# Held-out products in the middle of the value parts, three sign tiles moved to ScalarE, and the sum of a head's parts behind a later tile

## The reference

```python
q_proj, k_proj = one scalar per token and head (two linear layers with a gelu, then centred and scaled)
Z = concatenate(k_proj, q_proj); sort; cumsum; unsort
context = 2 * sum_k relu(Zq - Zk) * (v_k - mean v)        # what the sorted sums come to
norm    = sum_k |Zq - Zk|, at least 1e-4
out     = context / norm
```

## Time and profile before

| what | us |
|---|---|
| median of three runs | 1379.29 (1377.48 to 1381.62) |
| the profiled execution | 1386.35 |
| its span | 1385.0 |
| PE busy in it | 1080.4 (78%) |
| DVE busy in it | 960.1 (69%) |
| ACT busy in it | 818.6 (59%) |
| POOL busy in it | 354.9 (26%) |
| ACT sign tiles, 224 | 429.9 |
| DVE sign tiles, 288 | 352.7 |
| PE matmuls on the signs, 8192 | 398.3 |

### The profile page before, as it was taken

One profiled execution on the slowest core, in us unless ns is written; L12 is line 12 of the kernel. 1 busy time (PEld: TensorE's weight loads), 2 busy tenths in 40 slices (PEclk: granted clock), 3 DMA queues, 4 the chain that ended last, 5 costly groups with the idle time before them and its releaser, 6 DMA issues. The chain is left out here.

```text
span 1385.0 us, 30980 instructions
## 1 busy us (share of the span) xinstructions
PE 1080.4 (78%) x12566; PEld 932.0 (67%) x12566; DVE 960.1 (69%) x1709; ACT 818.6 (59%) x957; POOL 354.9 (26%) x381
## 2 busy tenths in 40 slices
PE   5365689798898899979998897665548948983797
PEld 3254686598888887658888886554348845652797
DVE  5111686889999995889999996255626647843465
ACT  7111454699999954489999996143413326660332
POOL 3745001100000000200004401571644421345344
PEclk9689699899999999979999999795669979966799
DMA  8953400311212100012123213554243450013343
GB/s 252 340 149 122 157 1 0 74 63 63 93 63 94 63 2 0 4 62 94 63 74 113 90 67 101 199 199 145 89 135 104 120 179 1 1 47 108 112 119 100
DMA packets 83824, 133.72 MB, mean 97 GB/s; under 512 B 14083, under 2 KB 70403, under 8 KB 79043
## 3 DMA queue, kind: packets, MB, share of 16 engines
q1 hardware_dynamic: 65440, 91.27, 20.9%
q0 software_dynamic: 12960, 35.60, 7.1%
q10 hardware_dynamic: 5286, 4.88, 1.1%
HBM read 84.18 MB, written 47.54 MB: 95 GB/s over the span
## 5 line engine op out<-in xcount | busy, mean ns | idle before, releaser
L1655 ACT ACTIVATE b_signs<-b_q_everywhere,normed 128x2048 bf16<-128x2048 f32 x224 | 429.9, 1993 | 13.4 <-PE banks L1537 13.0
L1537 PE MATMUL banks<-b_value_parts,b_signs 128*128 128x102 bf16 x8192 | 398.3, 209 | 46.1 <-DVE b_signs L1872 39.6
L1537 PEld LDWEIGHTS banks<-b_value_parts,b_signs 128*128 128x128 bf16 x8192 | 377.9, 98 | 64.4 <-DVE b_signs L1872 49.1
L1872 DVE TENSOR_SCALAR b_signs<-b_q_everywhere,normed 128x2048 bf16<-128x2048 f32 x288 | 352.7, 1279 | 4.7 <-PE banks L1537 4.6
L850 POOL DMA_INDIRECT moe_slots<-normed,slot_of_token x128 | 135.7, 1060 | 39.1 <-issue 35.2
L1924 POOL MEMSET b_value_parts<- 128x256 bf16 x2 | 2.6, 1310 | 404.6 <-PE banks L1385 404.6
L415 PE MATMUL banks<-identity 128*128 128x128 f32 x264 | 45.7, 351 | 53.7 <-issue 24.3
L379 DVE BATCH_NORM_STATS2 ln_stats<-residual 128x6 f32<-128x256 f32 x192 | 71.4, 417 | 17.1 <-SPq L2147 9.7
L415 PEld LDWEIGHTS banks<-identity 128*128 128x128 f32 x264 | 44.2, 264 | 54.5 <-issue 33.5
L406 ACT ACTIVATE normed<-residual,ln_shift,ln_rstd 128x256 f32<-128x256 f32 x128 | 67.9, 592 | 11.9 <-DVE ln_shift L401 11.8
L487 PE MATMUL banks<-identity,normed 128*128 128x128 f32 x256 | 51.8, 338 | 25.5 <-ACT normed L406 21.1
(11 more groups left out here) (292 smaller groups left out, 2299.3 us busy)
## 6 DMA issues: line engine op xcount, KB each, us to landing
b_q_everywhere<-q_rows SPq DMA_DIRECT2D x32, 1024.0 KB
normed<-expert_rows SPq DMA_DIRECT2D x6, 1024.0 KB, 10.0
d_rows<-moe_slots SPq DMA_DIRECT2D x39, 129.5 KB
f_rows<-moe_slots SPq DMA_DIRECT2D x39, 129.5 KB
moe_slots<-a_empty SPq DMA_DIRECT2D x8, 518.0 KB, 10.3
a_rows<-moe_slots SPq DMA_DIRECT2D x16, 259.0 KB
c_rows<-moe_slots SPq DMA_DIRECT2D x16, 259.0 KB
expert_rows<-a_empty SPq DMA_DIRECT2D x1, 4096.0 KB
```

Of the source, the lines that this page charges most:

```text
L1537: ins = nc.tensor.matmul(banks[qt // QPB][:, qt % QPB * VP:(qt % QPB + 1) * VP], t.SG[:, (hh * TB + kt) % RING, qt * P:(qt + 1) * P], t.VO ...
L1655: nc.scalar.activation(t.SG[:, g % RING, :], t.QB[:, hh % 2, :], ACT.Sigmoid, bias=t.NKT[:, kt, hh % H:hh % H + 1], scale=STEEP).then_inc( ...
L1872: nc.vector.tensor_scalar(t.SG[:, g % RING, :], t.QB[:, hh % 2, :], t.KTM[:, kt, hh % H:hh % H + 1], 1.0, ALU.is_gt, ALU.mult).then_inc(s. ...
```

## The change

`WARM_SENT` goes from 16 to 28 and `WARM_ROWS` from 12 to 16. In heads 6, 12 and 15 tile 15 is made by ACT and not by DVE. The sum of a head stands behind tile 4 and not tile 2 of the next head. The fifth context step of head 15 stands behind the loop, ahead of the last sum. The held-out matmuls stand in `pe_parts` at n = 2, with DVE's five operations at n = 4 of its loop over the pairs, and three new blocks of 8 idle matmuls stand in `pe_parts` at n = 4, 6 and 8, in bank 4. ACT gets one small sigmoid behind its first six copies of the parts.

```diff
-WARM_SENT, WARM_ROWS, WARM_HEADS, WARM_PAIR = 16, 12, 28, 4
+WARM_SENT, WARM_ROWS, WARM_HEADS, WARM_PAIR, WARM_PARTS = 28, 16, 28, 4, 8
-DVE_KT = tuple(t for t in range(TB) if t not in ACT_KT)
+EVEN_HEADS = (6, 12, H - 1)
+def act_tiles(h):
+    return ACT_KT + (TB - 1,) if h in EVEN_HEADS else ACT_KT
+def dve_tiles(h):
+    return tuple(t for t in range(TB) if t not in act_tiles(h))
+def act_made(hh):
+    return sum(len(act_tiles(i % H)) for i in range(hh))
+def dve_made(hh):
+    return TB * hh - act_made(hh)
@@ sp_attention
-                nc.sync.wait_ge(s.sign_d, len(DVE_KT) * (hh - 1))
-                nc.sync.wait_ge(s.sign_a, len(ACT_KT) * (hh - 1))
+                nc.sync.wait_ge(s.sign_d, dve_made(hh - 1))
+                nc.sync.wait_ge(s.sign_a, act_made(hh - 1))
@@ pe_parts, the end of the loop over n
+        if n == 2:
+            pe_held(k, batch)
+        if n in (4, 6, 8):
+            if n == 4:
+                nc.tensor.wait_ge(s.held, batch + 1)
+            pe_warm(k, k.bank[4], WARM_PARTS)
@@ pe_held
-    nc.tensor.wait_ge(s.nkt, batch + 1)
     nc.tensor.wait_ge(s.qtm, batch + 1)
+    nc.tensor.wait_ge(s.ones_set, batch + 1)
+    nc.tensor.wait_ge(s.kz_third, batch + 1)
@@ pe_head
-        nc.tensor.wait_ge(s.ones_set, batch + 1)
-        nc.tensor.wait_ge(s.kz_third, batch + 1)
-        pe_held(k, batch)
     if hh >= 2:
         nc.tensor.wait_ge(s.sum, hh - 1)
-    if h == 1:
-        nc.tensor.wait_ge(s.held, batch + 1)
@@ act_prepare, ahead of the loop over the pairs
+    nc.scalar.activation(t.ZS[:, 1:2], k.EPS[0:H, 0:1], ACT.Sigmoid)
     for n in range(PAIRS + 1):
@@ dve_attention
-            for kt in DVE_KT:
+            for kt in dve_tiles(h):
                 dve_sign(k, hh, kt)
-                if h == 0 and kt == 6:
-                    dve_held(k, batch)
-                if h and kt == 2:
+                if h and kt == 4:
                     dve_sum(k, hh - 1)
                 for group in made:
-                    if kt in CONTEXT_KT:
+                    if kt in CONTEXT_KT and (h, kt) != (H - 1, CONTEXT_KT[-1]):
                         dve_context(k, batch, group, CONTEXT_KT.index(kt))
...
+        dve_context(k, batch, len(TOGETHER) - 2, len(CONTEXT_KT) - 1)
         dve_sum(k, batch * H + H - 1)
@@ dve_prepare, in the loop over the pairs
+        if n == 4:
+            dve_held(k, batch)
         if n == 2:
```

More of the change, by code:

```diff
@@ L1531, in pe_head @@
                                  t.HELD3[:, h, :].unsqueeze(1).broadcast_to([P, QPB, 6]), start=False, stop=False)
-        if kt in ACT_KT:
-            nc.tensor.wait_ge(s.sign_a, len(ACT_KT) * hh + ACT_KT.index(kt) + 1)
+        if kt in act_tiles(h):
+            nc.tensor.wait_ge(s.sign_a, act_made(hh) + act_tiles(h).index(kt) + 1)
         else:
-            nc.tensor.wait_ge(s.sign_d, len(DVE_KT) * hh + DVE_KT.index(kt) + 1)
+            nc.tensor.wait_ge(s.sign_d, dve_made(hh) + dve_tiles(h).index(kt) + 1)
         for qt in range(TB):
@@ L1576, in act_attention @@
         for h in range(H):
-            for kt in ACT_KT:
+            for kt in act_tiles(h):
                 act_sign(k, batch * H + h, kt)
@@ L1729, in dve_prepare @@
             if i == 0 and batch:
-                nc.vector.wait_ge(s.sign_a, len(ACT_KT) * H * batch)
+                nc.vector.wait_ge(s.sign_a, act_made(H * batch))
             z = t.Z[:, q, ch * BANK:(ch + 1) * BANK]
@@ L1865, in dve_sign @@
     g = hh * TB + kt
-    if kt == DVE_KT[0]:
+    if kt == 0:
         nc.vector.wait_ge((s.qb_in0, s.qb_in1)[hh % 2], 16 * (hh // 2 + 1))
```

## The result

The kernel after took 1370.39 us (median of 5 runs, 1366.56 to 1371.59), the one before 1380.7 in the same comparison (5 runs). The ratio is 0.9937, 95% interval 0.9921 to 0.9952, so 8.7 us faster, 6.6 to 10.9. Against 1379.3 that is 1370.6: faster, as forecast, and 3.6 us short of the forecast, inside the range. The profiled execution took 1370.63, its span 1369.4.

The account below looks back on a forecast made before the run. DVE was taken to bound the heads, ACT those at a batch's start. Savings of 5.6 and 7.4 us made 13.0, less 0.7 gave 12.3, so 1379.3 would become 1367.0 us (chance 0.58), range 1361 to 1374.5.

Parts of the forecast that it names:

- The bound: Heads: DVE holds up the stretch, 41.66 us per three heads against ACT's 39.8; after the change ACT leads heads 0 to 2.
- That DVE carries its lead: Heads: with the sum behind tile 4, DVE starts a head at best 0.9 us ahead of ACT, up to the next context head.
- Rival 2: Heads: DVE's lead is lost at the ring, three heads cost 41.66 as before, some 3 us a batch remain: 1373; chance 0.08.
- The heads' size: Heads of both batches: summed path from ACT's first sign to the last sum, 219.65 us in batch 0.
- The 0.7 that I took off for missed meetings: Whole sum: 0.7 us deducted for places where three engines miss each other by a few tenths.
- The start: Parts ahead of the heads: DVE's first sign 0.9 us later, at 276.5, and ACT's at 276.6 without a load.
- The load and the sigmoid at nothing: Parts: table load and small sigmoid hold ACT about 1.5 us, made up in its wait for PE; price nothing, or 1.5.
- The drain: ACT's table switch: by the page another 1.28 us beside the load, holding ACT up to 2.9, 1 us worse per batch.
- rival 5: ACT's table: a copy brings the old table back, the sigmoid is loaded twice, 1.3 us a batch: 1370; chance 0.02.
- Rival 1: Parts: late ACT, held-out matmuls at 2.95 and DVE's wait not made up, 4.5 us a batch: 1374; chance 0.17.
- Rival 3: Stages behind the heads: longer idle blocks keep the higher clock, about 2.5 us in each of two stages: 1362; chance 0.10.
- Rival 4: Heads 1 to 11 of batch 1: PE waits at tile 5 for the later sum, 1.2 us each: 1387; chance 0.05.

Follow-up runs that it names:

- tiles_only: Kernel before with the moved tiles of heads 6, 12 and 15 and moved fifth context step, sum left behind tile 2: heads 1.14 and 2.86 us shorter.
- even_6_12: Kernel after with head 15's last tile given back to DVE: 0.1 us a batch longer.
- held_plain: Kernel after with the held-out matmuls reading neighbouring columns of a constant: start of the parts to DVE's first sign 30.03 us instead of 31.71.
- after_no_sig: Kernel after without the small sigmoid, table load again ahead of ACT's first sign: attention 2.8 us longer than in a repeat of the kernel after.
- warm_only: Kernel before with only the idle blocks of WARM_SENT and WARM_ROWS longer (28 and 16 passes): ratio 0.9994.
- same_again: Kernel before, unedited, run once more: heads the same to 0.02 us, 517.0 us behind the last sum, median of its comparison 1358.8 us.
- the three starred kernels: Follow-up kernels starred in a table of stretches, because they hold about 1.4 us of a lower clock in the second prepare.
- both_late: Kernel after with the small sigmoid one step later and DVE's held-out operations one pair later: ratio 0.9933 to the kernel before.

## Why the prediction was right, and where it was not

- *The bound* (DVE with context steps, ACT in the first heads) held, but for the end of the last head. DVE's terms came out as read from the earlier trace rows: 16.74 for 16.7, 15.54 for 15.5, 12.53 for 12.53. From the sum of head 2 to that of head 14 it took 164.78 us, by my terms 164.64. Heads 3 to 8 took 82.39 (319.34 to 401.73) against 83.34 before.
- *That DVE carries its lead* to the next context head was right, and tiles_only shows that it is the later sum that lets it. Rival 2 did not come about.
- *The heads' size* was too good. From ACT's first sign I had 219.65 and 226.15 us; it took 220.77 and 227.82. In batch 0, 0.3 of the 1.1 lies in the first three heads, 0.1 between, and 0.7 in the last, 13.21 from sum to sum instead of 12.5 (14.65 less three signs, and 1.45): the step and the tile were both counted in full, and even_6_12 shows that beside the step the tile gives 0.1. What DVE's sum of work leaves out is that ACT ends this head: its last tile is done at 496.31 (488.64 + 7.67), 1.0 behind DVE's last sign (495.28), and PE's last tile stands right behind it (496.41). Before that the ring had held ACT for 0.53 and 0.54 us, in heads 5 and 11, which I had given nothing, with 1 us as the bound. How much of the 0.7 comes from that no run shows. In batch 1, 0.8 lies before the sum of head 8, where ACT is the path, 0.2 between, 0.7 again in the last head. Together 2.8 us. The 0.7 that I took off for missed meetings was a quarter of it.
- *The start* was the other mis-sized term. I expected ACT's first sign 0.86 earlier in each batch; it came 0.10 earlier in both. DVE's wait and operations, which I put at 0.9 out of 0.4 to 1.7, cost 1.57. The step that failed is the one in which held-out matmuls at the higher clock take 1.5 us "if they follow the clock": they took 2.95, the other bound. With quick matmuls (held_plain) the 1.57 is gone. Together 1.5 us. These two terms make 4.3 us, from 13.0 to 8.7.
- *The load and the sigmoid at nothing*: right (0.20 for the sigmoid, as taken). after_no_sig gives the load 1.4 a batch.
- *The drain* that the page "ScalarE: Activation LUTs" of the Trainium skill puts at a switch of table ("What ACT_TABLE_LOAD costs"): no run shows one as time. The sigmoid starts 0.01 us behind the load's end, the load 0.02 behind the copy ahead of it. By the rule of the table sets, from the same page of the Trainium skill, a copy brings no second load; the trace agrees, ACT's first sign has none. With that rival 5 falls.
- *Rival 1* (the parts give it back) was right that the held-out matmuls take 2.95 and that DVE's wait for them is not made up, and wrong on ACT's 1.5, which is. Its price of 4.5 a batch was three times too high. Its 1374 and my 1367 enclose the 1370.6.
- *Rival 3* (the clock) fell by warm_only and by the data's matmuls. The clock fell in 873 to 874, between the last passes, and not 2.5 us behind the block's end as I had carried over from before; it was low before the data in either case. The stages behind the heads differ by 6 us between the two profiles, which my text would have taken for the clock. same_again shows that this mark was no mark: before itself took 542.8 us there in one comparison and 517.0 in another, and the runs with the long blocks (519.0 to 525.5) are no shorter there than those with the short ones (517.0 to 524.6).
- *Rival 4* fell: in batch 1 no head shows 1.2 more from sum to sum, the most is 0.7 (14.12 for 13.43, from the sum of head 7 to that of head 8, where ACT is the path), and DVE's tile 12 waits for PE in heads 0 and 2 alone, 0.41 and 0.36.
- *Luck*: the two mis-sized terms go the same way, so that the forecast wasn't saved by misses that cancel. The 0.7 taken off had the right sign, but stood for no wait in particular.

## What to carry to other kernels

When two engines share a row of tiles and one also carries irregular work, the place of its first wait for the other decides how much lead it can carry. In batch 0 moving tiles without moving that wait gave nearly all of them back in the next two heads; in batch 1, where the engine was late for another reason, it did not. Read how far apart the columns of a small matmul's operand lie before pricing it by the clock. And judge a small edit by a stretch that repeats to a tenth of a us, not by whole spans.

## What the runs showed of the hardware

- Sixteen matmuls with 96 moving columns took 2.95 us at the granted clocks 0.50 and 1.00 alike when the columns lie 17 bf16 elements apart, and 0.84 us when they are neighbours (held_plain, clock 1.00).
- TensorE's clock can dip for a moment where the kernels run the same instructions. Between the sum of batch 0 and the scaling of the k row in batch 1 the three starred kernels took 77.0 to 77.1 us and the others 75.6 to 75.7. Eight us from both_late (clock 0.82) and from held_plain (1.00), at the same place behind the sum of batch 0:

```profile
523.68:531.68 8.00, 8.00 (x38) 6.88 (x37) 2.89 (x5) 5.47 (x8) 0.00 (x0) 0.82 0.00 0
```
```profile
523.25:531.25 8.00, 8.00 (x48) 6.07 (x45) 2.79 (x5) 6.13 (x9) 0.00 (x0) 1.00 0.00 0
```

  What sets it off stays open; no run here varies it alone.
- A long idle block is not issued evenly. In after its first 49 passes ran in 7.53 us, the last seven came in ones and threes with gaps of up to 1.72 us in which PE waited for nothing that the profile shows. The 24 passes more, some 2.6 us at the higher clock by the prediction, made the block 5.3 us longer (862.50 to 874.21, against 6.43 us before), and still moved nothing here.
